# A planned order of work laid out anew: the self-attention block of the loop, half blocks of values, and an earlier transpose in the second step

## The chip, the core and the metric

The kernel runs on one core of a Trainium2 chip. The metric is the device time of one launch in microseconds. TensorE does the matrix products and transposes, VectorE (DVE) and ScalarE (ACT) read its PSUM banks, GpSimd (POOL) works on SBUF alone, SyncE (SP) issues most DMAs. Each engine works through a queue of its own in order and is held by semaphore waits.

## The reference

For 64 sequences of 128 tokens by 128 features, in float32:

```
x = x + tanh(gx) * cross_attention(layernorm(x), ctx)      # 16 heads of 8, 120 context tokens
h = rms(layernorm(x)); q, k = rms by head; v = h @ wv.T    # causal self-attention, 16 heads of 8
ffn_x = layernorm(x) + self_attention(h) @ wo.T            # the first 32 output features set to 0
moe = sum of 4 experts, two of them chosen by gate         # the first 32 output features set to 0
x = x + tanh(gf) * (ffn_x + moe)
```

Expert 0 has one hidden layer, expert 1 a gated one, expert 2 three, expert 3 two. All experts are computed for all tokens and weighted by `gates`.

## The kernel before

The sequences are worked in 16 groups of 4 (`G = 4`, 512 tokens). Work on a group is cut into five parts that lie one group apart in a software pipeline: N (layer norm, cross queries, keys, values), A (cross attention), B (norm, self queries, keys, values), D (self attention, gate, first expert layers), M (second and later expert layers, store). A step t does N of group t+1, A of group t, B of t-1, D of t-2 and M of t-3. Steps -1 to 2 are the ramp, steps 3 to 14 are twelve rounds of one hardware loop (`LOOP = (3, NG - 1)`), step 15 follows the loop's order without part N, and steps 16 to 18 are the tail.

The order of a loop step is written out by hand as a list, `SCHEDULE = self_attention() + second_experts() + cross_attention() + first_experts()`. Each entry is (part, work, index, ring). Every engine walks the same list and picks out the works in which it has a share, so the list sets the order in all five queues. `ring` names the PSUM banks that a work takes in turn: "w" is four banks, "s2" and "f" are both the pair s2a and s2b, "pv" and "t" are one bank each. Before a work writes its bank, TensorE waits until the use before has been read out (`st.drains`).

The works that matter here:

- `exact` (s2): two products of exact scores for sequence b; ScalarE takes the exponential of each into `probs` (L951). For part D, GpSimd masks each pair of results (L818), after a small `tick` (L817).
- `estimate` (s1): four products into the four "w" banks at once (L1302, L1306); TensorE waits for all four banks first. VectorE reduces each to maxima (L1092). After the last estimate of a part, `mT` transposes the maxima (L1315), ScalarE copies them, and SyncE stores them into a row of the stacked queries (L676); the first exact score of that part waits for this DMA.
- `values` (pv): 32 small products for one sequence (L1363), which wait for the exponentials, in part D for the masks. After each second sequence come oT (transpose; VectorE divides, L1131, L1133), nT and wo (L1376; VectorE adds, L1148).
- `qk`, `squares`, `sums`, `root`, `scale`, `qT`, `kT` of part B: the products (L1274) are copied by ScalarE, squared by GpSimd (L829), summed by VectorE (L1067), rooted by ScalarE (L905), scaled by VectorE (L1071, L1073), transposed by TensorE (L1225), and split by ScalarE (L856, L861) and VectorE (L985, L993).
- `down`: sixteen products of an expert's last layer (L1389); VectorE adds them into `ym` in four instructions (L1121).
- `D out` is yb (L1155), `N stats` and `N norm` are the statistics and xn (L1007), with a power by GpSimd between them (L760).

Numbers such as D13 below mean part D, sequence 1, quarter 3. The ramp's steps have lists of their own: `third_group()` is step 1, `fourth_group()` is step 2 and takes its first half from `self_attention()` without part M.

## Time and profile before

| | us |
|---|---|
| median of 3 runs | 1071.3 (1071.01 to 1073.17) |
| the profiled execution's own time | 1074.17 |
| its span, first to last instruction | 1072.5 |
| TensorE busy in the span | 1009.0 (94%) |
| VectorE busy | 788.7 (74%) |
| ScalarE busy | 736.5 (69%) |
| GpSimd busy | 338.1 (32%) |

A round of the loop takes 62.5 to 62.7 us. TensorE's busy time counts the latency of products that overlap, so that a gap of some tenths between products may not show in it. An idle time in brackets is that of the engine just before the instruction, with what ended it.

### The profile page before, as it was taken

What the parts mean: (1) busy time and instruction counts of PE and PEld (TensorE: products, weight loads), DVE (VectorE), ACT (ScalarE), POOL (GpSimd) and SP (SyncE); (2) the same over time, 40 slices, a digit from 0 to 9 for tenths busy, and PEclk for the clock granted to TensorE, in tenths of its full rate; (3) what the DMA queues carried; (4) which work ended last, traced back from release to release, by engine and by line L of the source; (5) the groups of instructions that cost most, each with busy time, mean ns of one, the idle gap of its engine ahead of it and who ended that gap; (6) DMA issues with size and microseconds to landing.
All of it is one profiled execution on the core that took longest, in us unless ns stands there. A gap on an engine that the chain in (4) does not pass through costs nothing.

```text
span 1072.5 us, 26205 instructions
## 1 busy us (share of the span) xinstructions
PE 1009.0 (94%) x8649; PEld 627.7 (59%) x8649; DVE 788.7 (74%) x2172; ACT 736.5 (69%) x1334; POOL 338.1 (32%) x463
## 2 busy tenths in 40 slices
PE   6768799999999999999999999999999999999898
PEld 5445556556565655656565565656556565656565
DVE  8546878777877877787787778778777877774723
ACT  6465767676777767677776767777676777767453
POOL 5613424141422414142241414224141422404130
PEclk9868999999999999999999999999999999999999
DMA  7424432233342224334222443422244342221200
GB/s 233 127 72 158 133 104 89 88 130 128 115 134 96 87 88 130 128 115 135 97 86 88 130 128 115 135 96 87 88 130 128 115 135 96 82 79 49 83 1 20
DMA packets 77317, 114.28 MB, mean 107 GB/s; under 512 B 7776, under 2 KB 40160, under 8 KB 77152
## 3 DMA queue, kind: packets, MB, share of 16 engines
q1 hardware_dynamic: 76800, 111.53, 32.1%
q10 hardware_dynamic: 480, 2.26, 0.6%
q8 instruction: 23, 0.38, 0.1%
q14 instruction: 14, 0.11, 0.0%
HBM read 58.97 MB, written 53.74 MB: 105 GB/s over the span
## 4 chain that ended last, share of the span: by engine, by line
PE 65%; DVE 14%; ACT 11%; issue 6%; DMA 2%; SPq 1%; POOL 0%; ACTq 0%; DVEq 0%; POOLq 0%
PE ps_pv L1363 9%; PE ps_w L1389 9%; PE ps_s2a L1342 7%; PE ps_s2b L1342 5%; PE ps_s2a L1401 5%; PE ps_s2b L1408 4%; ACT probs L951 4%; PE ps_t L1225 4%; PE ps_w L1408 3%; PE ps_w L1274 3%; DVE mpadA L1092 3%; PE ps_t L1376 2%; PE ps_w L1225 2%; PE ps_w L1306 2%; PE ps_w L1302 2%
## 5 line engine op out<-in xcount | busy, mean ns | idle before, releaser
L951 ACT ACTIVATE probs<-ps_s2a 120x512 f32<-120x512 f32 (+1 forms) x256 | 153.4, 599 | 76.6 <-PE ps_s2a L1342 68.5
L1092 DVE TENSOR_REDUCE mpadB<-ps_w 128x4 f32<-128x512 f32 x240 | 148.8, 683 | 22.7 <-PE ps_w L1306 22.7
L1092 DVE TENSOR_REDUCE mpadA<-ps_w 128x4 f32<-128x480 f32 x224 | 131.5, 650 | 38.1 <-PE ps_w L1306 38.1
L951 ACT ACTIVATE probs<-ps_s2b 120x512 f32<-120x512 f32 (+1 forms) x256 | 153.5, 599 | 0.0
L818 POOL TENSOR_SCALAR_AFFINE_SELECT probs<-probs 128x1024 f32<-128x1024 f32 x128 | 139.8, 1092 | 0.0
L1389 PE MATMUL ps_w<-W,hid 128*128 128x96 f32 x976 | 121.3, 278 | 1.0 <-DVE split_k L985 0.9
L1389 PEld LDWEIGHTS ps_w<-W,hid 128*128 128x128 f32 x976 | 113.8, 192 | 10.4 <-issue 4.9
L786 POOL TENSOR_TENSOR rB<-vrB,neg_half 128x4 f32<-128x4 f32 x16 | 16.1, 1008 | 204.5 <-DVE veB L978 204.5
L1342 PE MATMUL ps_s2a<-qdA,kstA 128*120 128x512 f32 x128 | 70.2, 548 | 9.2 <-DMA qdA<-scratch_Aq 4.8
L1401 PE MATMUL ps_s2a<-hid,W 128*128 128x512 f32 x152 | 74.4, 604 | 0.0
L1121 DVE SCALAR_TENSOR_TENSOR ym<-ps_w,gates,ym 128x96 f32<-128x96 f32 x184 | 45.7, 311 | 38.6 <-PE ps_w L1389 38.6
L955 ACT ACTIVATE oT<-ps_pv 128x512 f32<-128x512 f32 x64 | 38.3, 598 | 50.9 <-PE ps_pv L1363 50.9
L1342 PE MATMUL ps_s2a<-qdB,kstB 128*128 128x512 f32 x128 | 64.6, 505 | 7.6 <-ACT probs L951 2.1
L1363 PE MATMUL ps_pv<-probs,VA 120*18 120x128 f32 x2048 | 71.2, 282 | 0.0
L947 ACT ACTIVATE hid<-ps_s2a 128x512 f32<-128x512 f32 x73 | 43.7, 599 | 40.0 <-PE ps_s2a L1401 30.9
L1363 PE MATMUL ps_pv<-probs,VB 128*18 128x128 f32 x2048 | 68.4, 274 | 0.0
L1363 PEld LDWEIGHTS ps_pv<-probs,VA 120*18 120x18 f32 x2048 | 51.9, 100 | 24.2 <-issue 22.9
L817 POOL TENSOR_TENSOR tick<-one 128x1 f32<-128x1 f32 x128 | 24.9, 194 | 117.5 <-ACT probs L951 113.2
L1363 PEld LDWEIGHTS ps_pv<-probs,VB 128*18 128x18 f32 x2048 | 50.5, 97 | 17.2 <-issue 16.9
L958 ACT ACTIVATE onT<-ps_t 128x256 f32<-128x256 f32 x64 | 24.5, 384 | 51.6 <-PE ps_t L1225 51.6
L1342 PE MATMUL ps_s2b<-qdA,kstA 128*120 128x512 f32 x128 | 59.3, 463 | 0.0
L825 POOL TENSOR_TENSOR ym<-yb,one 128x128 f32<-128x128 f32 x16 | 6.4, 398 | 166.2 <-DMA out_x<-ym 166.2
(279 smaller groups left out, 2170.3 us busy)
## 6 DMA issues: line engine op xcount, KB each, us to landing
scratch_Aq<-split_q SPq DMA_DIRECT2D x48, 256.0 KB, 2.4
qdA<-scratch_Aq SPq DMA_DIRECT2D x64, 192.0 KB
scratch_Bq<-split_q SPq DMA_DIRECT2D x48, 256.0 KB, 2.4
scratch_Bk<-split_k SPq DMA_DIRECT2D x48, 256.0 KB, 2.9
qdB<-scratch_Bq SPq DMA_DIRECT2D x64, 192.0 KB
kstB<-scratch_Bk SPq DMA_DIRECT2D x64, 192.0 KB
scratch_Ak<-split_k SPq DMA_DIRECT2D x48, 240.0 KB, 2.3
kstA<-scratch_Ak SPq DMA_DIRECT2D x64, 180.0 KB
```

The costliest lines, as they stand in the source:

```text
L818: pool.affine_select(out=tile, in_=tile, compare_op=ALU.is_ge, fill=0.0, base=0, pattern=[[0, 2 * HT], [1, P]], channel_multiplier=-1).the ...
L947: nc.scalar.activation(hid[:, HID_AT[index[0]] + index[1], :], bank[:], ACT.Gelu).then_inc(done, 1)
L951: nc.scalar.activation(probs[0:k, slot_of(part, *index), :], bank[0:k, :], ACT.Exp, scale=SCALE if part == "A" else 1.0).then_inc(done, 1)
L955: nc.scalar.activation(oT[:], bank[:], ACT.Copy).then_inc(done, 1)
L1092: nc.vector.tensor_reduce(pair[:, :, c, b % 2] if halves else mneg[p][:, :, c, b], bank[:, 0:HT * k].rearrange("p (h k) -> p h k", h=HT), ...
L1121: ins = nc.vector.scalar_tensor_tensor(out=ym[:, b, KEEP:P], in0=bank[:, b * UP:(b + 1) * UP], scalar=gates[:, b, e:e + 1], in1=y[:, b, KE ...
L1225: ins = nc.tensor.transpose(psum[st.bank[key]][:, b * P:(b + 1) * P], of(b), identf[:])
L1342: mm(o, kst[p][:, c, b * k:(b + 1) * k], qd[p][:, :, c, b * P:(b + 1) * P], start=True, stop=True).then_inc(done, 1)
L1363: ins = mm(psum[st.bank[last]][32 * j:32 * j + VS, at:at + P], VB[p][0:k, first:first + VS], probs[0:k, slot_of(part, b, c), j * P:(j + 1) ...
L1389: ins = mm(bank[:, b * UP:(b + 1) * UP], hid[:, HID_AT[h] + k, b * P:(b + 1) * P], w[f"down{index[1]}"][:, k * UP:(k + 1) * UP], start=k = ...
L1401: ins = mm(bank[:], w[name][:, k * HID + c * P:k * HID + (c + 1) * P], hid[:, HID_AT[h] + k, :], start=k == 0, stop=k == chunks[-1])
L1408: mm(bank[:], w[name][:, c * P:(c + 1) * P], xfT[:], start=True, stop=True).then_inc(done, 1)
```

## The change

Nothing is computed differently, and no instruction is added but for the waits of the half blocks. What changes is order:

- `values` of part D is split into `early_values` (quarters 0 and 1) and `late_values` (quarters 2 and 3), 16 products each, laid between other works.
- `down(0)` is split into `head(0)` (sequences 0 and 1) and `rest(0)`; VectorE still adds all four in one go, after `rest`.
- In `self_attention()` the estimates A0 and A1 come later, and A2 moves behind the output product wo0, into `second_experts()`; so does the whole of e2_l2.
- In `second_experts()` the B transposes qT and kT come before the second output product wo1, `out` and `squares` of part D; in VectorE's queue the splits of queries and keys therefore come before wo1's addition and yb.
- Step 1 begins with B's hT, ahead of the first exact scores of A. In step 2, estimate A2 comes behind wo0 as in the loop, and A3 behind `scale` and oT1.

```
 def self_attention():
-    return (... exact("D", 0, 0) + one("B", "hT") + down(1) + exact("D", 0, 2)
-            + one("B", "qk", 0) + one("B", "qk", 1) + one("B", "qk", 2) + one("B", "qk", 3)
-            + exact("D", 1, 0) + estimate("A", 0) + exact("D", 1, 2)
-            + one("B", "squares", 0, None) + values("D", 0)
-            + exact("D", 2, 0) + estimate("A", 1) + exact("D", 2, 2)
-            + values("D", 1) + one("B", "sums", 0, None) + down(0)
-            + exact("D", 3, 0) + one("D", "oT", 0, "t") + estimate("A", 2) + exact("D", 3, 2)
-            + one("A", "base", 0, None) + values("D", 2) + one("D", "nT", 0, "t") + one("B", "root", 0, None))
+    return (... exact("D", 0, 0) + one("B", "hT") + down(1)
+            + exact("D", 0, 2) + one("B", "qk", 0) + one("B", "qk", 1) + early_values("D", 0)
+            + exact("D", 1, 0) + one("B", "qk", 2) + one("B", "qk", 3) + late_values("D", 0)
+            + exact("D", 1, 2) + one("B", "squares", 0, None) + estimate("A", 0) + early_values("D", 1)
+            + exact("D", 2, 0) + head(0) + late_values("D", 1)
+            + exact("D", 2, 2) + one("B", "sums", 0, None) + rest(0) + one("D", "oT", 0, "t")
+            + exact("D", 3, 0) + early_values("D", 2) + estimate("A", 1) + one("D", "nT", 0, "t") + late_values("D", 2)
+            + exact("D", 3, 2) + one("A", "base", 0, None) + one("B", "root", 0, None))
 def second_experts():
-    return (fill("M", "e2_l2", 0) + one("D", "wo", 0, "t") + one("B", "scale", 0, None) + fill("M", "e2_l2", 1)
-            + estimate("A", 3) + values("D", 3) + fill("M", "e3_up", 0) + one("D", "oT", 1, "t") + fill("M", "e3_up", 1)
-            + one("N", "stats", 0, None)
-            + one("D", "nT", 1, "t") + one("A", "mT") + fill("M", "e2_l3", 0) + one("N", "norm", 0, None) + one("D", "wo", 1, "t")
-            + one("D", "out", 0, None) + one("B", "qT") + one("B", "kT") + one("D", "squares", 0, None)
-            + fill("M", "e2_l3", 1, "w"))
+    return (one("D", "wo", 0, "t") + early_values("D", 3) + estimate("A", 2) + fill("M", "e2_l2", 0) + one("B", "scale", 0, None)
+            + late_values("D", 3) + fill("M", "e2_l2", 1) + estimate("A", 3) + fill("M", "e3_up", 0) + one("D", "oT", 1, "t")
+            + fill("M", "e3_up", 1) + one("N", "stats", 0, None) + one("A", "mT") + fill("M", "e2_l3", 0) + one("D", "nT", 1, "t")
+            + one("N", "norm", 0, None) + one("B", "qT") + one("B", "kT") + one("D", "wo", 1, "t")
+            + one("D", "out", 0, None) + one("D", "squares", 0, None) + fill("M", "e2_l3", 1, "w"))
 def third_group():
-    return (exact("A", 0, 0) + exact("A", 0, 2) + one("A", "mL", 0, "t") + exact("A", 1, 0) + values("A", 0) + one("B", "hT")
-            + exact("A", 1, 2) + one("B", "qk", 0) ... + one("B", "qk", 3)
-            + one("B", "squares", 0, None) + one("B", "copy", 0, None)
+    return (one("B", "hT") + exact("A", 0, 0) + exact("A", 0, 2)
+            + one("B", "qk", 0) ... + one("B", "qk", 3) + one("A", "mL", 0, "t")
+            + exact("A", 1, 0) + exact("A", 1, 2) + one("B", "squares", 0, None) + one("B", "copy", 0, None) + values("A", 0)
             + exact("A", 2, 0) + one("B", "sums", 0, None) + one("B", "root", 0, None) + exact("A", 2, 2)
 def fourth_group():
-            + one("D", "wo", 0, "t") + estimate("A", 3) + values("D", 3) + one("D", "oT", 1, "t") + one("A", "mT")
-            + one("B", "scale", 0, None) + one("D", "nT", 1, "t") + one("N", "stats", 0, None) + one("D", "wo", 1, "t")
+            + one("D", "wo", 0, "t") + early_values("D", 3) + estimate("A", 2) + one("B", "scale", 0, None) + late_values("D", 3)
+            + one("D", "oT", 1, "t") + estimate("A", 3) + one("A", "mT") + one("D", "nT", 1, "t") + one("N", "stats", 0, None) + one("D", "wo", 1, "t")
```

The new functions (`head` writes half of the bank that `down` 0 takes, and signals nothing; `rest` signals):

```
+def early_values(part, b):
+    return values(part, b, 0, PACK)
+def late_values(part, b):
+    return values(part, b, PACK, NT)
+HEADED = (0,)
+def head(e):
+    return one("M", "head", e, None)
+def rest(e, ring="w"):
+    return fill("M", "down", e, ring)
+def down(e, ring="w"):
+    return (head(e) if e in HEADED else []) + rest(e, ring)
...
-                        for b in range(G):
+                        for b in range(0 if work == "head" or e not in HEADED else G // 2, G // 2 if work == "head" else G):
```

The tail's lists call `down` under its new form, in the order they had.

## Rows read from the trace of the kernel before

**Rows 1.** The page, its first line
```profile
span 1072.5 us, 26205 instructions
...
```

**Rows 2.** One whole step of the loop: us, busy us by engine, TensorE's clock, DMA
```profile
...
403.07:465.61 62.54, 61.21 (x536) 38.03 (x536) 48.85 (x136) 45.40 (x84) 19.37 (x25) 1.00 0.34 111
...
```

**Rows 3.** Timeline of TensorE in the loop step from 403.07: start, us, [idle before]
```profile
...
409.63 0.50 PE L1342 MATMUL ps_s2a<-qdB,kstB 128*128 128x512 f32 x1
...
417.93 0.38 PE L1306 MATMUL ps_w<-kdA,qTbA 32*128 32x480 bf16 x4 [0.32 <-DVE ym L1121]
...
428.04 0.44 PE L1225 MATMUL ps_t<-identf,on 128*128 128x128 f32 x2
...
430.57 1.04 PE L1225 MATMUL ps_w<-identf,qk 128*128 128x128 f32 x8
...
438.67 0.40 PE L1302 MATMUL ps_w<-causal_k,causal_q 32*128 32x512 bf16 x4
...
```

**Rows 4.** Timeline of VectorE, the same step
```profile
...
414.89 1.21 DVE L1067 TENSOR_REDUCE hs<-sq 128x128 f32<-128x1024 f32 x1
416.79 0.99 DVE L1121 SCALAR_TENSOR_TENSOR ym<-ps_w,gates,ym 128x96 f32<-128x96 f32 x4 [0.69 <-PE ps_w L1389]
...
422.52 0.36 DVE L1148 TENSOR_TENSOR x<-ps_t,x 128x192 f32<-128x192 f32 x1 [1.76 <-PE ps_t L1376]
...
424.92 2.34 DVE L1092 TENSOR_REDUCE mpadA<-ps_w 128x4 f32<-128x480 f32 x4
...
430.52 1.11 DVE L1007 TENSOR_SCALAR xn<-xt,mvA,rsA 128x128 f32<-128x128 f32 x4 [1.13 <-POOL rsA L760]
...
432.02 1.54 DVE L1155 SCALAR_TENSOR_TENSOR yb<-x,tg,xc 128x512 f32<-128x512 f32 x1
...
434.15 0.73 DVE L985 SCALAR_TENSOR_TENSOR split_k<-ps_w,vc,split_k 128x512 fp32r<-128x512 f32 x1
...
436.66 0.99 DVE L1121 SCALAR_TENSOR_TENSOR ym<-ps_w,gates,ym 128x96 f32<-128x96 f32 x4
439.30 2.49 DVE L1092 TENSOR_REDUCE mpadB<-ps_w 128x4 f32<-128x512 f32 x4 [1.65 <-PE ps_w L1306]
```

**Rows 5.** Timeline of GpSimd, the same step
```profile
...
411.68 1.09 POOL L818 TENSOR_SCALAR_AFFINE_SELECT probs<-probs 128x1024 f32<-128x1024 f32 x1
412.74 1.89 POOL L829 TENSOR_TENSOR sq<-qk 128x1024 f32<-128x1024 f32 x1
...
```

**Rows 6.** Timeline of ScalarE, the same step
```profile
...
435.43 0.60 ACT L951 ACTIVATE probs<-ps_s2a 120x512 f32<-120x512 f32 x1
...
```

**Rows 7.** Timeline of all engines in the second step (t=1)
```profile
...
53.22 1.11 DVE L1032 TENSOR_SCALAR hb<-x,mvB,rB 128x128 f32<-128x128 f32 x4 [1.13 <-POOL rB L786]
...
58.90 1.12 PE L1225 MATMUL ps_w<-identf,hb 128*128 128x128 f32 x4
...
63.39 1.89 POOL L829 TENSOR_TENSOR sq<-qk 128x1024 f32<-128x1024 f32 x1 [9.22 <-ACT qk L896]
...
68.87 0.95 DVE L1071 RECIPROCAL hr<-hr 128x128 f32<-128x128 f32 x1
...
71.13 1.12 PE L1225 MATMUL ps_w<-identf,qk 128*128 128x128 f32 x4 [5.38 <-DVE qk L1073]
```

**Rows 8.** Timeline of all engines in the third step (t=2)
```profile
...
107.60 1.21 DVE L1067 TENSOR_REDUCE hs<-sq 128x128 f32<-128x1024 f32 x1
...
112.64 2.35 DVE L1092 TENSOR_REDUCE mpadA<-ps_w 128x4 f32<-128x480 f32 x4
...
115.71 0.55 SPq L676 DMA_DIRECT2D qdA<-mTA  x1
...
118.73 0.75 PE L1342 MATMUL ps_s2a<-qdA,kstA 128*120 128x512 f32 x1 [1.24 <-issue]
...
126.24 0.40 PE L1302 MATMUL ps_w<-causal_k,causal_q 32*128 32x512 bf16 x4 [0.33 <-ACT xnT L870]
...
```

**Rows 9.** Busy time and clock in eight microseconds of the third step
```profile
...
116.00:124.00 8.00, 5.40 (x26) 4.39 (x26) 7.01 (x23) 5.95 (x10) 2.03 (x2) 0.79 0.16 54
...
```

More of the change, by code:

```diff
@@ L89, in estimate, with values @@
     return [(part, "s1", (b, c), rings[c]) for c in range(NT)]
-def values(part, b):
-    return [(part, "pv", (b, c), "pv" if b % 2 and c == NT - 1 else None) for c in range(NT)]
+def values(part, b, first=0, last=NT):
+    return [(part, "pv", (b, c), "pv" if b % 2 and c == NT - 1 else None) for c in range(first, last)]
+def early_values(part, b):
+    return values(part, b, 0, PACK)
+def late_values(part, b):
+    return values(part, b, PACK, NT)
 def one(part, work, index=0, ring="w"):
@@ new lines, in head @@
+def head(e):
[4 more added lines that the diff above has]
+    return (head(e) if e in HEADED else []) + rest(e, ring)
+def self_attention():
+    return (one("N", "load", 0, None) + one("N", "ctx", 0, None) + exact("D", 0, 0) + one("B", "hT") + down(1)
+            + exact("D", 0, 2) + one("B", "qk", 0) + one("B", "qk", 1) + early_values("D", 0)
[5 more added lines that the diff above has]
+            + exact("D", 3, 2) + one("A", "base", 0, None) + one("B", "root", 0, None))
@@ L236, in last_self_keys @@
             + one("D", "squares", 2, None) + estimate("B", 1) + fill("M", "e2_l3", 1)
[L237 to L238 removed]
+            + down(2, "pv") + estimate("B", 2) + one("D", "norm", 2, None) + one("B", "init", 0, None) + one("B", "copy", 0, None)
+            + one("D", "xfT", 0, "t") + down(3, "pv") + one("M", "store", 0, None) + one("B", "v", 0, "f") + one("D", "logits", 0, "t")
             + fill("D", "e1_w1", 0) + fill("D", "e1_w2", 0) + one("D", "keep", 0, None) + estimate("B", 3)
@@ L261, in last_experts @@
 def last_experts():
-    return (fill("M", "down", 1, "t") + fill("M", "e2_l2", 0) + fill("M", "e2_l2", 1) + down(0) + fill("M", "e2_l3", 0) + fill("M", "e2_l3", 1)
+    return (down(1, "t") + fill("M", "e2_l2", 0) + fill("M", "e2_l2", 1) + down(0) + fill("M", "e2_l3", 0) + fill("M", "e2_l3", 1)
             + fill("M", "e3_up", 0, "w") + fill("M", "e3_up", 1, "w") + down(2) + down(3) + one("M", "store", 0, None))
@@ L1378, in step @@
                         ins.then_inc(done, 1)
-                    elif work == "fill" and index[0] == "down":
-                        h = DOWN_OF[index[1]]
-                        if index[1] in (0, 1):
-                            sources = st.settled(*(("f",) if st.parts == "M" and index[1] == 1 else ("w", "f")))
-                        else:
-                            sources = st.drains([("M", "fill", (h, k)) for k in range(2)])
-                        for b, v in merged(sources, st.drains([], key)):
-                            pe.wait_ge(drained[b], v)
-                        for b in range(G):
+                    elif work == "head" or work == "fill" and index[0] == "down":
+                        e = index if work == "head" else index[1]
+                        use, h = ("M", "fill", ("down", e)), DOWN_OF[e]
+                        if work == "head" or e not in HEADED:
+                            if e in (0, 1):
+                                sources = st.settled(*(("f",) if st.parts == "M" and e == 1 else ("w", "f")))
+                            else:
+                                sources = st.drains([("M", "fill", (h, k)) for k in range(2)])
+                            for b, v in merged(sources, st.drains([], use)):
+                                pe.wait_ge(drained[b], v)
+                        for b in range(0 if work == "head" or e not in HEADED else G // 2, G // 2 if work == "head" else G):
                             for k in range(2):
-                                ins = mm(bank[:, b * UP:(b + 1) * UP], hid[:, HID_AT[h] + k, b * P:(b + 1) * P],
-                                         w[f"down{index[1]}"][:, k * UP:(k + 1) * UP], start=k == 0, stop=k == 1)
-                        ins.then_inc(done, 1)
+                                ins = mm(psum[st.bank[use]][:, b * UP:(b + 1) * UP], hid[:, HID_AT[h] + k, b * P:(b + 1) * P],
+                                         w[f"down{e}"][:, k * UP:(k + 1) * UP], start=k == 0, stop=k == 1)
+                        if work == "fill":
+                            ins.then_inc(done, 1)
                     elif work == "fill" and index[0] in ("e2_l2", "e2_l3", "e3_up"):
```

7 lines of the change are left out of this document (1 added, 6 removed).

## The prediction

> **What bounds the kernel now.** I read the page first: the span is 1072.5 us [rows 1]. Then the windows, step by step: a loop step takes 62.5 us, TensorE is busy for 61.2 of them at full clock, VectorE for 48.9 [rows 2]. That looks like a TensorE bound, but the busy time counts overlapping latencies, so I read the chain of waits through one step and then the four timelines beside each other. In the stretch that the change lays out anew, TensorE stops for others: for the addition of `down` 0 before estimate A2, for the divided output before nT1, and only then runs on to qT and to the first causal estimate B0 [rows 3]. VectorE stops twice, 0.69 us before ym and 1.76 us before wo0's addition, and 1.65 us before B0's maxima [rows 4]. So neither is full; the step's length is set by a chain that changes engines. From B0 onwards the order is unchanged, and what the change does to a loop step is how much earlier or later B0 starts than at 438.67 [rows 3].
>
> **The loop step, worked through in the new order.** I lay the new order on the old clock, with the step's first exact score at 403.07.
>
> TensorE first. Before D12 it now has all 32 value products of sequence 0 and no estimate: the values cost 1.0 us, the estimate and a stop 0.5, so D12 starts at about 410.1 and not at 409.63 [rows 3]. D13 follows it at streaming distance, so its mask starts only 0.3 us later than at 411.68, near 412.0. GpSimd's squares stand behind that mask, and come at 413.0 for 412.74 [rows 5]; they take 1.89 us and end at 414.9. `sums` on VectorE waited for VectorE itself before; it now waits for the squares and starts at 414.94 for 414.89 [rows 4]. The early start of the values costs nothing there, since A0's four maxima are done by 413.4.
>
> From here VectorE is the chain, because A1 as well as A2 and A3 now stand behind `sums`. The distances from start to start, all from [rows 4] or the neighbouring starts of the same timeline: sums 1.14, ym 0.91 (416.79 to the next start), division and product of oT0 0.73, maxima A1 2.26 (the 2.34 of four less their overlap with the next), and so A1 is read at 420.0. TensorE can issue A2 only when A1's last bank is free, which costs VectorE 0.35, then A2 2.26, addition of wo0 and the scaling together 2.40 (422.52 to 424.92). That is 414.94 + 1.14 + 0.91 + 0.73 + 2.26 + 0.35 + 2.26 + 2.40 = 424.99 for A3, against 424.92. VectorE's two stops of 0.69 and 1.76 us are gone, and one more set of maxima, 2.26 us, has taken their place. The masks, exponentials and head/rest of `down` 0 lie beside this: late D1 is free at 413.1, `rest` is filled at 415.3, while VectorE gets to ym at 416.1. If that cover went, each tenth late at ym would be a tenth at B0. TensorE meanwhile waits some 0.4 us for the mask before early D1, 0.6 for ym before A1 (D2's first half and D3 are queued behind it only in part), 0.4 for nT0; it is off the chain, so these cost nothing now.
>
> A3 to xn is 5.60 us (424.92 to 430.52), the same works in the same order, so xn starts at 430.6. On TensorE, mT now stands before e2_l3 and nT1 behind it. mT waits for A3's maxima until 427.4; then 1.72 for e2_l3's first half and 0.27 for nT1 bring qT to 429.55, against 430.57 [rows 3]: one microsecond earlier, since wo1 has moved behind. ScalarE's four casts end 0.9 us earlier, at 432.7, and its first exponential of A00 comes at 434.7 for 435.43 [rows 6], there held by e2_l3's second half, whose products end at 432.6.
>
> VectorE then does the splits before wo1's addition and yb. xn ends at 431.7, the query split runs to 432.3, and the key split must wait for ScalarE until 432.73. After it: key split to ym 2.51 (434.15 to 436.66), addition and yb 0.36 + 1.54, ym 0.99, which is 432.73 + 2.51 + 1.90 + 0.99 = 438.1; B0 waits for ym's bank and starts at 438.3. TensorE and ScalarE alone would have allowed 438.1. So a loop step gains 438.67 - 438.3 = 0.4 us. No DMA decides: the store of mT's row is issued at about 428.0 and takes 3.0 us as in [rows 8] (115.71 to 118.73), A00 comes at 432.6; the load of x is issued 0.3 us later behind `base` and has until 428. The bounds: if ScalarE's casts or the start of A2 come sooner than I have it, 0.6 (TensorE's and ScalarE's limit); if each stop adds a tenth or the squares are late by 0.3, nothing or a loss of 0.1. Twelve rounds and step 15 make thirteen: -4.8 us, between -8 and +1.5.
>
> **Step 2.** It takes the same list without M. The anchor is the same: squares at 105.6, sums at 107.6 [rows 8]. Before, all maxima but A3's were done or next; A3's were read from 112.64 for 2.35 us, to 115.0, ahead of the scaling. Now VectorE has after sums: oT0 0.73, A1 2.26, addition 0.3 and a gap of 0.35, A2 2.26, scaling 2.12, oT1 0.73, A3 2.34, from 107.6 + 1.14. That ends at 119.8, later by 4.8. Here no e2_l2 or e3_up fills TensorE, and mT, its DMA and A00 follow at the distances of before, 0.72 to the issue and 3.02 to A00: 123.6 for 118.73. The B transposes are queued behind A00 on TensorE, and everything up to B0 at 126.24 behind them; ScalarE's and VectorE's splits had some slack there (they waited for xn), which gives back 0.3 to 0.6. I take +4.5, between +2.5 and +6.
>
> Clock: in 116 to 124 it averages 0.79 of full [rows 9], and the exact score A00 took 0.75 us. The new order leaves TensorE idle for some 4 us before mT, so the low level (1.2 GHz) may reach on into B0. The Trainium skill, "TensorE: Matmul & The Clock Gate", section "HAM oscillation", says that idle stretches between bursts of matmuls bring the half clock back and each must be paid anew. By that rule step 2 would cost more than these 4.5 us; by the rows, where the stretch was at 0.79 anyway, it costs no more. The sum goes by the rows; the rule is a rival below.
>
> **Step 1.** hT can start when hb ends, 53.22 + 1.11 = 54.33; it started at 58.90 [rows 7]. Now A00, ready at 53.19, is queued behind it, and so are A's exponentials, by 1.4 us. The four qk end near 61.2, squares at 61.65 for 63.39. But the root stands on ScalarE behind the exponentials of A20 and A21, and these behind mL's row, whose transpose has moved behind qk. I get A21's exponential to 65.9, a table load of 1.28 and the root to 67.6, the reciprocal at 67.65 for 68.87, and qT as much before 71.13. The gain is 1.2 us, between 0 and 2.
>
> **Other edits.** `down` in its new form issues the same products in the tail: nothing. Split values add waits that are long met: nothing.
>
> **Sum.** -4.8 + 4.5 - 1.2 = -1.5 us, on the span 1072.5, so 1071.0. The profiled execution took 1074.17 in all, 1.7 above its span and 2.9 above the median of the timed runs, 1071.3; taken off that median, the forecast is 1069.8 us. A measurement of this kernel tells about 0.2%, 2.1 us, from no change: this is a change of 0.14%, within it.
>
> **Rivals.**
> - *VectorE does not bind the loop step.* If the wait for ScalarE before the key split vanishes and the estimates are issued early, a step gains 0.6 to 0.9. For it: qT is a whole microsecond earlier, and VectorE stood idle 1.65 us before B0. Against: the order puts A1 behind sums. With 0.75 a step, 9.8, and steps 1 and 2 as above: 1064.8 us.
> - *The squares set a later chain.* Slower: GpSimd's mask of D13 stands before the squares, and the squares before the masks of D2. If TensorE reaches D13 0.8 us later than before instead of 0.3 (each half block restarting after its wait), sums starts 0.5 later, the step loses 0.1, and with steps 1 and 2 the time is 1071.3 + 1.3 + 3.3 = 1075.9. It decides from a delay of 0.4 us, where the gain of a step is gone.
> - *The clock in step 2.* As the skill's page would have it: nT1, wo1, A00, qT and the estimate at half speed cost 1.5 more, 1071.3 us.
> - *Nothing at all in the loop* is no case of its own; it lies between the first two.
>
> **How the numbers follow.** Forecast, 0.40: 1067.5 to 1072.5, of this 0.12 faster, 0.27 the same, 0.01 slower. No VectorE bound, 0.32, all faster. Late squares, 0.20: 0.18 slower, 0.02 the same. Clock, 0.08: 0.01 faster, 0.05 the same, 0.02 slower. Together faster 0.45, same 0.34, slower 0.21. The range leaves a tenth on each side: the first rival's 1064.8 with its larger half, and the slower one's centre: 1063.5 to 1075.5. For the likeliest alone it is 1067.5 to 1072.5.
>
> **What would show it.** In the changed loop step: the distance from the first exact score to B0, 35.2 us for 35.6; VectorE without a stop of over 0.4 us from sums to A3's end, and its ym of `down` 2 ending just before B0; sums about 11.9 us after the step's first score. In step 2: A00 nearly 5 us later after sums than 11.1 us, with VectorE solid before it. In step 1: hT at once after hb, and ScalarE's root as the last thing before the scaling. The prediction is wrong if B0 waits for something else than ym, if sums slips by 0.4 us or more, or if step 2 doesn't move.

## The result and the profile of the changed kernel

The changed kernel is slower: 1082.95 us, median of 4 runs (1081.08 to 1084.22), against 1071.78 for the kernel before (4 runs, 1071.01 to 1073.17), a ratio of 1.0098 with an interval of 1.0082 to 1.0114. The forecast was 1069.8 within 1063.5 to 1075.5, so the time lies 7.5 us outside the range. The page of the changed kernel's profiled execution, 1081.08 us in all:

```profile
span 1079.2 us, 26181 instructions
...
PE 1009.3 (94%) x8649; PEld 622.4 (58%) x8649; DVE 791.3 (73%) x2172; ACT 733.6 (68%) x1334; POOL 339.0 (31%) x463
...
```

One loop step, from its first exact score to that of the next, the two steps of the ramp from the start of one hT to the start of the next, and the eight microseconds of [rows 9] (us, busy us by engine, the clock, DMA):

```profile
...
405.21:468.31 63.10, 61.43 (x536) 37.70 (x537) 49.06 (x136) 45.21 (x84) 19.40 (x25) 1.00 0.35 111
52.09:91.21 39.12, 28.63 (x245) 17.37 (x246) 24.50 (x66) 23.15 (x44) 5.91 (x5) 0.83 0.26 87
91.21:152.66 61.45, 50.55 (x453) 30.04 (x453) 44.40 (x116) 39.58 (x75) 20.04 (x25) 0.89 0.36 116
116.00:124.00 8.00, 6.48 (x26) 5.17 (x25) 4.41 (x18) 5.86 (x11) 2.09 (x2) 0.54 0.02 4
...
```

The loop step took 62.54 us [rows 2] and takes 63.10, step 2 took 56.13 from hT to hT (96.28 to 152.41) and takes 61.45. From the end of hb to the next hT, step 1 took 41.95 and takes 39.18. From the hT of step 3 to that of step 16, thirteen intervals of which eleven grew by 0.52 to 0.58 and the two at the ends by 0.3, the sum is 6.5 us. Over the two profiled executions: 6.5 + 5.3 - 2.8 - 2.3 (the ramp up to hb, where the orders are the same) - 0.1 (the tail) = 6.7 us, the difference of the spans. The ramp's 2.3 and part of the 2.8 are scatter between executions (below); with step 1 at the 1.2 us that its order gives and the ramp at nothing, the parts make 10.6; the medians differ by 11.2.

TensorE in the loop step (start, us, what ended the stop before it):

```profile
...
412.54 0.50 PE L1364 MATMUL ps_s2a<-qdB,kstB 128*128 128x512 f32 x1
...
419.72 0.38 PE L1328 MATMUL ps_w<-kdA,qTbA 32*128 32x480 bf16 x4 [0.42 <-DVE ym L1143]
420.35 0.44 PE L1247 MATMUL ps_t<-identf,on 128*128 128x128 f32 x2 [0.25 <-DVE on L1155]
...
422.92 0.38 PE L1328 MATMUL ps_w<-kdA,qTbA 32*128 32x480 bf16 x4
...
427.63 0.38 PE L1328 MATMUL ps_w<-kdA,qTbA 32*128 32x480 bf16 x4
...
430.45 0.33 PE L1337 MATMUL ps_w<-identf,mpadA 128*128 128x128 f32 x1
...
432.65 1.04 PE L1247 MATMUL ps_w<-identf,qk 128*128 128x128 f32 x8
...
441.36 0.40 PE L1324 MATMUL ps_w<-causal_k,causal_q 32*128 32x512 bf16 x4 [0.28 <-DVE ym L1143]
...
```

VectorE, the same step:

```profile
...
417.45 1.22 DVE L1089 TENSOR_REDUCE hs<-sq 128x128 f32<-128x1024 f32 x1 [1.48 <-POOL sq L851]
...
420.21 2.35 DVE L1114 TENSOR_REDUCE mpadA<-ps_w 128x4 f32<-128x480 f32 x4
...
423.33 2.35 DVE L1114 TENSOR_REDUCE mpadA<-ps_w 128x4 f32<-128x480 f32 x4 [0.51 <-PE ps_w L1328]
...
428.04 2.35 DVE L1114 TENSOR_REDUCE mpadA<-ps_w 128x4 f32<-128x480 f32 x4 [0.24 <-PE ps_w L1328]
...
435.85 0.75 DVE L1007 SCALAR_TENSOR_TENSOR split_k<-ps_w,vc,split_k 128x512 fp32r<-128x512 f32 x1 [0.41 <-ACT split_k L883]
...
437.95 1.63 DVE L1177 SCALAR_TENSOR_TENSOR yb<-x,tg,xc 128x512 f32<-128x512 f32 x1
...
440.31 0.99 DVE L1143 SCALAR_TENSOR_TENSOR ym<-ps_w,gates,ym 128x96 f32<-128x96 f32 x4
...
```

GpSimd, the same step:

```profile
...
415.52 1.90 POOL L851 TENSOR_TENSOR sq<-qk 128x1024 f32<-128x1024 f32 x1
...
```

The step begins at 405.21, and all distances below are from that start (403.07 before). D12 comes at 7.33 (forecast 7.03), the squares at 10.31 (9.67 before [rows 5]; forecast 9.93), sums at 12.24 (11.82 before [rows 4]; forecast 11.87), A3's maxima at 22.83 (21.85 before; forecast 21.92), qT at 27.44 (27.50 before [rows 3]; forecast 26.5), B0 at 36.15 (35.60 before; forecast 35.2). So the handing over of A3 is 0.9 us later than I had it, and everything behind it by as much: from A3's maxima to B0 the forecast had 13.3 us and the trace has 13.32. The second thing to see is TensorE between nT0 at 420.35 and A3's estimate at 427.63: no row there has a stop, while VectorE waits 0.51 and 0.24 us for the products of A2 and A3. The chain that I had put on VectorE lies on TensorE there.

Step 1, all engines:

```profile
...
64.89 0.40 ACT L927 ACTIVATE hr<-hs,rms_eps 128x128 f32<-128x128 f32 x1
...
65.32 0.95 DVE L1093 RECIPROCAL hr<-hr 128x128 f32<-128x128 f32 x1 [0.30 <-ACT hr L927]
...
67.59 1.09 PE L1247 MATMUL ps_w<-identf,qk 128*128 128x128 f32 x8 [2.47 <-DVE qk L1095]
...
```

Step 2, all engines:

```profile
...
102.76 1.22 DVE L1089 TENSOR_REDUCE hs<-sq 128x128 f32<-128x1024 f32 x1 [1.46 <-POOL sq L851]
...
113.10 2.34 DVE L1114 TENSOR_REDUCE mpadA<-ps_w 128x4 f32<-128x480 f32 x4
...
115.50 0.48 PE L1337 MATMUL ps_w<-identf,mpadA 128*128 128x128 f32 x1 [4.20 <-DVE mpadA L1114]
...
119.10 0.75 PE L1364 MATMUL ps_s2a<-qdA,kstA 128*120 128x512 f32 x1 [1.05 <-issue]
...
126.48 0.40 PE L1324 MATMUL ps_w<-causal_k,causal_q 32*128 32x512 bf16 x4 [0.31 <-ACT xnT L892]
...
```

### The profile page after: what moved, and what is told of

It reads as the page before. It is cut to its first block, busy times and chain, and to the rows that moved or that the text cites. A ratio compares the mean times of both kernels' runs of the same rounds, so it can differ in the third digit from the quotient of the medians.

```text
span 1079.2 us, 26181 instructions
## 1 busy us (share of the span) xinstructions
PE 1009.3 (94%) x8649; PEld 622.4 (58%) x8649; DVE 791.3 (73%) x2172; ACT 733.6 (68%) x1334; POOL 339.0 (31%) x463
## 4 chain that ended last, share of the span: by engine, by line
PE 62%; DVE 17%; ACT 9%; issue 8%; POOL 3%; DMA 0%; DVEq 0%; ACTq 0%; POOLq 0%
PE ps_pv L1385 10%; PE ps_w L1413 6%; PE ps_s2a L1364 6%; PE ps_s2a L1426 5%; PE ps_s2b L1433 4%; PE ps_s2b L1364 3%; PE ps_t L1247 3%; PE ps_s2b L1426 3%; PE ps_w L1433 3%; PE ps_w L1296 3%; DVE mpadA L1114 3%; PE ps_w L1328 2%; DVE ym L1143 2%; POOL sq L851 2%; ACT probs L973 2%
## 5 line engine op out<-in xcount | busy, mean ns | idle before, releaser
L1385 PE MATMUL ps_pv<-probs,VB 128*18 128x128 f32 x2048 | 79.9, 277 | 2.1 <-POOL probs L840 2.0
L1385 PE MATMUL ps_pv<-probs,VA 120*18 120x128 f32 x2048 | 69.0, 276 | 0.1
L1385 PEld LDWEIGHTS ps_pv<-probs,VB 128*18 128x18 f32 x2048 | 45.9, 97 | 37.9 <-issue 22.8
L969 ACT ACTIVATE hid<-ps_s2b 128x512 f32<-128x512 f32 x60 | 35.8, 597 | 30.2 <-PE ps_s2b L1426 26.1
L1364 PE MATMUL ps_s2b<-qdA,kstA 128*120 128x512 f32 x128 | 56.2, 439 | 0.0
```

The source lines that it names most:

```text
L969: nc.scalar.activation(hid[:, HID_AT[index[0]] + index[1], :], bank[:], ACT.Gelu).then_inc(done, 1)
L1364: mm(o, kst[p][:, c, b * k:(b + 1) * k], qd[p][:, :, c, b * P:(b + 1) * P], start=True, stop=True).then_inc(done, 1)
L1385: ins = mm(psum[st.bank[last]][32 * j:32 * j + VS, at:at + P], VB[p][0:k, first:first + VS], probs[0:k, slot_of(part, b, c), j * P:(j + 1) ...
```

## The experiments

Each kernel is read by the same clock: the distance from one hT on TensorE to the next, which within one execution repeats to some hundredths of a microsecond over the inner steps of the loop, where the interval of a ratio is some 2 us wide. "Stops" are the stretches of TensorE's timeline between the step's first exact score and B0 in which no matmul runs, added up; what is left of that distance I call TensorE's own time; a wait shorter than the latency of the matmul before it hides in there (exact scores that start 0.49 us apart and not 0.34), so it is no fixed amount of work: late_estimates below, which cuts no block, has 1.0 us more of it than tail_on_before. The columns are good to 0.02 us.

```
kernel             loop step   first score to B0 = stops + own   step 2
before                 62.55       35.61           0.98   34.63   56.13
changed                63.09       36.14           1.16   34.98   61.45
tail_on_before         62.35       35.42           0.99   34.43   56.09
whole_values           63.19       36.26           1.43   34.83   60.78
halves_of_1_2          63.09       36.17           1.46   34.71   61.96
estimates_forward      63.03       36.10           1.29   34.81   58.15
late_estimates         64.70       37.79           2.33   35.46   56.12
```

**Which part costs.** step1_alone is the kernel before with the new third_group and nothing else.

> The kernel before with the new order of step 1 alone (hT first). In the changed kernel the stretch from the end of hb in step 1 to hT of step 2 was 39.2 us against 41.9, so the new order of step 1 is expected to give 2.8 us by itself: 1069, ratio 0.9975. If that gain needs the changed loop, or was the chance of one execution, the ratio is 1.000. My prediction had 1.2 us for it. All loop steps must stay at 62.55 us.

It took 1069.67 us, ratio 0.9984 (0.997 to 0.9999), and its loop step is 62.56. The new step 1 gains 1 to 1.7 us (0.1 to 3.2 by the interval), and not the 2.8 of the two profiles. The end of hb to qT takes 15.72 us in it and 15.56 in the changed kernel, and 16.2 to 16.8 in the four kernels with the old step 1; all fifteen with the new one lie between 14.2 and 15.8, with 15.4 in the middle, so the order gives about 1.1 us there. From qT to the next hT the four take 22.6, 24.3, 24.4 and 25.2 us: that stretch is scatter.

step2_of_before is the changed kernel whose fourth_group has the old order (ramp_self_attention is the old list under a new name, and the lines behind it are the old ones too):

```
-    return (one("D", "mL", 0, "t") + of_parts("NABD", self_attention())
+    return (one("D", "mL", 0, "t") + of_parts("NABD", ramp_self_attention())
```

> The changed kernel with step 2 in the order of before (self-attention and what follows it up to A00), loop and step 1 changed. If step 2 costs 5.3 us as hT to hT of step 3 says (61.45 against 56.13), the time is 5 us under the changed kernel's, 1078, ratio to before about 1.0045 to 1.005. If the loss of step 2 is only the time won in step 1 that is given back at the next DMA or at the start of the loop, it stays near 1083. Loop steps stay at 63.09 us.

1079.31 us, ratio 1.0072 (1.0049 to 1.0094), step 2 at 56.18 for 61.45, the loop step unchanged at 63.09. Step 2 costs 3.6 us by the medians, 2.8 by the ratios, whose intervals are some 2 us wide to each side, and 5.3 by the profiles; the loop costs the rest. Step 2 scatters too: with the old order it took 56.1 to 56.2 us in six kernels and 57.2 in two (step1_and_tail, wo1_between), with the changed one 61.4, 61.45 and 62.15.

step2_a3_first keeps the new step 2 and puts A3 ahead of the scaling and of oT1 in it:

> The changed kernel with one thing moved, in step 2 only: estimate A3 ahead of scale and oT1, as before. If step 2's 5.3 us come through A3's maxima, mT, its DMA and A00, the stretch hT to hT of step 2 shrinks from 61.4 by the scaling and the division that A3 no longer waits for, by 2 to 3 us. If they come from the first half of the step (half blocks, masks), it stays at 61.

1084.35 us, ratio 1.0122 (1.0108 to 1.0137); step 2 takes 60.49, 1.0 less and not 2 to 3. mT comes 2.2 us earlier behind sums, but nT1 and wo1 are queued ahead of A00 on TensorE and wait for the divided output, which the scaling has moved back; so A00 comes only 0.94 us earlier behind sums. The time itself shows no gain.

**The new tail.** tail_on_before is the kernel before with the change's tail of second_experts alone:

```
-            + one("N", "stats", 0, None)
-            + one("D", "nT", 1, "t") + one("A", "mT") + fill("M", "e2_l3", 0) + one("N", "norm", 0, None) + one("D", "wo", 1, "t")
-            + one("D", "out", 0, None) + one("B", "qT") + one("B", "kT") + one("D", "squares", 0, None)
+            + one("N", "stats", 0, None) + one("A", "mT") + fill("M", "e2_l3", 0) + one("D", "nT", 1, "t")
+            + one("N", "norm", 0, None) + one("B", "qT") + one("B", "kT") + one("D", "wo", 1, "t")
+            + one("D", "out", 0, None) + one("D", "squares", 0, None)
```

> The kernel before with one part of the change alone: in second_experts the tail from stats on in the new order (mT, e2_l3's first half, nT1, norm, qT, kT, wo1, out). The block of exact scores and the estimates A0 to A3 stay where they were, steps 1 and 2 too. Theory T (the new tail by itself is right as the prediction had it, and what the change loses is that the block hands over A3 about 1.0 us later): A3's maxima stay 21.85 us behind the step's first exact score, mT and qT follow them at the changed kernel's distances (2.41 and 4.61 us), so qT at 26.5 and B0 8.7 us later at 35.2; a loop step takes 62.15 us for 62.55 and the kernel 5 us less, about 1066. Rival O (the tail order itself costs: the splits ahead of wo1's addition lengthen qT to B0 from 8.10 to 8.71 us, and qT does not come earlier, since xn, which waits for GpSimd's root, stands before the splits): a loop step of 62.9 to 63.1 us, the kernel 5 to 7 us longer than before. Between: no change, 62.5 to 62.6.

The loop step is 62.35 us, 0.20 shorter; 1069.4 us, ratio 0.9988 (0.9975 to 1.0001), so the time alone does not tell it from no change, and the step does. Its step from 521.96, TensorE:

```profile
...
548.67 1.04 PE L1224 MATMUL ps_w<-identf,qk 128*128 128x128 f32 x8
...
557.38 0.40 PE L1301 MATMUL ps_w<-causal_k,causal_q 32*128 32x512 bf16 x4 [0.27 <-DVE ym L1120]
...
```

qT is at 26.71 and B0 at 35.42; A3's maxima stayed at 21.85. The tail does what the prediction said, at half the size. By the table the gain is in TensorE's own time, 34.43 for 34.63, and not in its stops. wo1_first asks the reverse, the changed kernel with the old tail:

```
-            + fill("M", "e3_up", 1) + one("N", "stats", 0, None) + one("A", "mT") + fill("M", "e2_l3", 0) + one("D", "nT", 1, "t")
-            + one("N", "norm", 0, None) + one("B", "qT") + one("B", "kT") + one("D", "wo", 1, "t") + one("D", "out", 0, None)
+            + fill("M", "e3_up", 1) + one("N", "stats", 0, None) + one("D", "nT", 1, "t") + one("A", "mT") + fill("M", "e2_l3", 0)
+            + one("N", "norm", 0, None) + one("D", "wo", 1, "t") + one("D", "out", 0, None) + one("B", "qT") + one("B", "kT")
```

> The changed kernel with the second half of second_experts in the order of before: nT1 before mT, wo1's addition and yb before the splits of queries and keys. Theory A, the late maxima (A1 behind sums, A3 begins 0.98 us later from the step's start than before) are what costs, and qT before wo1 hides part of it: a loop step gets longer than 63.09 by 0.2 to 0.45, 3 to 6 us in all. Theory B, the place of the splits costs, since the key split waits 0.41 us for ScalarE with yb and ym behind it: a loop step gets shorter by up to 0.4, 5 us in all.

63.52 us a step, 1089.79 us in all, ratio 1.0168 (1.0144 to 1.0191). So the four corners are 62.55 (old, old), 62.35 (old block, new tail), 63.52 (new block, old tail), 63.09 (both new): the new block costs 0.74 with the new tail and 0.97 with the old one, which is the 0.98 by which A3 is late.

**Is VectorE the chain up to A3?** half_read takes work from VectorE alone: its maxima of A1 read half of the keys, so the stabilizer of that sequence's scores comes from half of them.

```
-    bank[:, 0:HT * k].rearrange("p (h k) -> p h k", h=HT),
+    bank[:, 0:HT * k].rearrange("p (h k) -> p h k", h=HT)[:, :, 0:k // 2 if (part, b) == ("A", 1) else k],
```

> The changed kernel, but VectorE reads only the first 60 of 120 keys for the four maxima of estimate A1, which takes about 1.1 us out of its queue between sums and A2 (so the maxima of sequence 1 are those of half its keys). Theory V, VectorE's queue alone is the chain from sums to A3, as the prediction had it: a loop step gets shorter by 0.5 to 0.9 us, 7 to 12 us in all. Theory T, TensorE's own run from nT0 to A3 (7.3 us without a stop, against 6.65 in my sum) is the chain, and VectorE waits for A2's and A3's products (0.51 and 0.24 us): the step stays within 0.1 us of 63.09.

The step stays at 63.08 (1081.04 us, ratio 1.0101, 1.0085 to 1.0117). VectorE in its step from 468.33:

```profile
...
483.32 1.34 DVE L1114 TENSOR_REDUCE mpadA<-ps_w 128x4 f32<-128x240 f32 x4
485.58 0.36 DVE L1170 TENSOR_TENSOR x<-ps_t,x 128x192 f32<-128x192 f32 x1 [0.91 <-PE ps_t L1398]
486.44 2.35 DVE L1114 TENSOR_REDUCE mpadA<-ps_w 128x4 f32<-128x480 f32 x4 [0.51 <-PE ps_w L1328]
...
491.15 2.35 DVE L1114 TENSOR_REDUCE mpadA<-ps_w 128x4 f32<-128x480 f32 x4 [0.23 <-PE ps_w L1328]
...
```

A1's maxima take 1.34 us for 2.34, the microsecond turns into a stop of 0.91 before wo0's addition, and A3's maxima start at 22.82, where they were. So VectorE's queue does not set A3 here: TensorE's run from nT0 to A3 does, and nT0 itself stands behind sums, ym and the division on VectorE.

**The value products in halves.** whole_values is the changed kernel with every `early_values` left out and every `late_values` whole.

> The changed kernel with the value products of part D whole, all at the place of the later half; the rest of the layout kept. Theory A1, the entries between half blocks of values and exact scores make TensorE late (an exact score after small value products takes 0.43 and not 0.23, half a block 0.56 and not 0.50), so that squares and the estimates A2 and A3 come late: a step gets 0.3 to 0.45 us shorter, 4 to 6 us in all, to about 1078. Theory A2, only the order on VectorE (A1 behind sums) counts: the step stays within 0.1 us of 63.09.

63.19 us a step, 1080.64 us, ratio 1.0089 (1.0066 to 1.0112): the halves don't cost more than they fill. What one costs by itself shows two_splits, the kernel before with two blocks of A cut where TensorE doesn't wait:

```
-    values("A", 2) + one("D", "logits")
+    values("A", 2, 0, PACK) + one("D", "logits") + values("A", 2, PACK, NT)
-    fill("D", "e1_w2", 0, "w") + values("A", 3)
+    values("A", 3, 0, PACK) + fill("D", "e1_w2", 0, "w") + values("A", 3, PACK, NT)
```

> The kernel before with two blocks of value products in cross_attention and first_experts cut in halves round another work (A2 round the logits, A3 round e1_w2's first half), where TensorE runs without a stop; nothing else moved. Theory H (a half block costs TensorE 0.1 to 0.3 us each time it is restarted, also where nothing waits): a loop step grows by 0.2 to 0.5 us, the kernel by 3 to 7 us. Rival (the cut costs nothing, the exact scores were longer only since they stood behind small products): within 0.05 us a step, the kernel the same within 1 us.

The step is 63.08 us, 0.53 more, and the kernel 1079.63, ratio 1.008 (1.006 to 1.01): two cuts cost as much as the whole change of the block and tail. A2's block and what follows it, whole in the kernel before:

```profile
...
574.16 1.07 PE L1363 MATMUL ps_pv<-probs,VA 120*18 120x128 f32 x32
575.16 1.05 PE L1264 MATMUL ps_w<-W,xfT 128*128 128x4 f32 x8
576.08 0.41 PE L1225 MATMUL ps_t<-identf,on 128*128 128x128 f32 x2
576.33 1.02 PE L1408 MATMUL ps_w<-xfT,W 128*128 128x512 f32 x2
...
```

and cut in two_splits:

```profile
...
574.78 0.63 PE L1363 MATMUL ps_pv<-probs,VA 120*18 120x128 f32 x16
575.35 1.05 PE L1264 MATMUL ps_w<-W,xfT 128*128 128x4 f32 x8
576.33 0.63 PE L1363 MATMUL ps_pv<-probs,VA 120*18 120x128 f32 x16
576.89 0.44 PE L1225 MATMUL ps_t<-identf,on 128*128 128x128 f32 x2
577.17 1.02 PE L1408 MATMUL ps_w<-xfT,W 128*128 128x512 f32 x2
...
```

From the start of the block to that of the product behind nT it takes 2.39 us for 2.17. The 32 products took 1.00, the two sixteens 0.57 and 0.56; the work behind each is slower too, the logits by 0.06 here. The other cut costs 0.22 on its own stretch and 0.10 ahead of it. I take 0.22 to 0.27 us a cut.

halves_of_1_2 is the changed kernel with sequences 0 and 3 whole at their late places.

> The changed kernel with the value products of sequences 0 and 3 whole at the places of their late halves; those of 1 and 2 stay in halves. Theory H (each split costs TensorE 0.22 us, and both of these stand in runs that set the chain: sequence 0's before the mask that releases the squares, sequence 3's between nT0 and A3): sums 0.22 us sooner, 12.02 us behind the step's first exact score, A3's maxima 0.44 us sooner, at 22.4, and a loop step of 62.65 us for 63.09. Rival L (the estimates' later places are the whole loss): a step of 63.05 to 63.1.

Not a hundredth: 63.09 us a step (1082.02 us, ratio 1.0087, 1.0067 to 1.0107). Half of the theory held, sums at 12.02 as expected. But now TensorE stops for VectorE before A2; its step begins at 534.45:

```profile
...
549.37 0.44 PE L1247 MATMUL ps_t<-identf,on 128*128 128x128 f32 x2 [0.25 <-DVE on L1155]
...
551.72 0.38 PE L1328 MATMUL ps_w<-kdA,qTbA 32*128 32x480 bf16 x4 [0.27 <-DVE mpadA L1114]
...
556.87 0.38 PE L1328 MATMUL ps_w<-kdA,qTbA 32*128 32x480 bf16 x4
...
```

A3's estimate is at 22.42, as in the changed kernel (427.63 - 405.21): the 0.22 won at sums is lost from nT0 on, 7.50 us for 7.28. The early half of sequence 3 (0.56) is gone from that run, the whole block is 0.44 longer than the late half was, and 0.34 comes back between wo0 and A2, as a wait for A1's maxima. That is also why half_read found nothing: with the halves in, VectorE is ready for A2 some 0.2 us before TensorE asks for it, and whoever shortens TensorE's run by more meets VectorE's (17.27 us from the step's start to A2's estimate here, released by A1's maxima, with sums 0.22 earlier, for 17.71 in the changed kernel). From A2's estimate to A3's, TensorE needs 5.15 us with a whole block between e2_l2's halves (1.91 + 1.00 + 1.92 + 0.32); my sum had only VectorE's 4.66 there.

**The estimates' places.** late_estimates has, on tail_on_before, the change's later places of A0 to A3 and wo0 alone; value blocks, down 0 and the four qk are whole where they were.

> The kernel before with the new tail (a loop step of 62.35 us) and the estimates A0 to A3 and wo0 at the later places of the change, but all value products whole and the qk blocks where they were; step 2 as before. Theory H (half blocks alone are the loss): a loop step within 0.1 us of 62.35. Rival L (the later places alone, since TensorE's own run from nT0 to A3 then stands behind the wait for ym): 62.7 to 63.1 us. Between the two, 62.5, both have a share.

64.70 us a step, 2.35 more than tail_on_before (1099.74 us, ratio 1.0254, 1.0229 to 1.0278), beyond both theories. TensorE in its step from 539.04:

```profile
...
545.60 0.50 PE L1353 MATMUL ps_s2a<-qdB,kstB 128*128 128x512 f32 x1 [0.49 <-ACT probs L962]
...
549.31 0.49 PE L1353 MATMUL ps_s2a<-qdB,kstB 128*128 128x512 f32 x1 [0.45 <-ACT probs L962]
...
554.44 0.38 PE L1317 MATMUL ps_w<-kdA,qTbA 32*128 32x480 bf16 x4 [0.25 <-DVE ym L1132]
...
557.32 0.68 PE L1387 MATMUL ps_t<-W,onT 128*128 128x96 f32 x4 [0.47 <-ACT onT L969]
...
```

Where an estimate stood between two exact scores, TensorE now waits for ScalarE to drain a bank; where wo0 had e2_l2 ahead of it, it waits for the cast onT. The estimates were the filling. So what the change does to the block is to take this filling out, at 2.35 us a step, and to put other filling in (halves of values, of qk and of down 0), which gives 1.6 back. Which of these gives it was asked by two more of the changed kernel, qk_together (four qk ahead of sequence 0's first values) and whole_down (down 0 whole at the place of its second half):

> The changed kernel with the four qk products together again behind qk 0 and 1, ahead of sequence 0's first value products; all else as changed. If the qk pairs fill the times in which TensorE would wait for ScalarE to drain the exact scores' banks (0.49 and 0.45 us in late_estimates), a loop step grows by 0.4 to 1.0 us from 63.09; if the value halves fill them as well, within 0.1 us.

> The changed kernel with down 0 whole at the place of its second half. If its first half fills a wait for ScalarE's drains or for the mask ahead of sequence 1's second value products, a loop step grows by 0.3 to 0.6 us from 63.09, and ym comes later behind sums; if sums and the squares ahead of it are what ym waits for anyway, within 0.1 us.

63.17 and 63.18 us a step, in one execution each (1084.23 and 1082.06 us): each alone is worth 0.1, like the value halves in whole_values. That they stand in for one another is the likeliest reading, since without all three it is 64.70; no run takes out two of them, and in whole_values the whole blocks still stand where the late halves did.

estimates_forward keeps the halves and puts the estimates back (A0 ahead of D12, A1 ahead of sums, A2 and A3 one place forward, mT two blocks forward, stats ahead of oT1):

> The half blocks of the change kept, but all four estimates one place forward: A0 ahead of D12, A1 ahead of sums, A2 and A3 where the change has A1 and A2, mT two blocks earlier. If the places of the estimates are what costs the change 0.54 us a step, and the half blocks cost little, a step takes 62.2 to 62.6 us, at or under the 62.55 of before, and the whole comes to 1064 to 1072. If the half blocks cost by themselves, it stays at or above 62.9.

63.03 us a step (1078.0 us in all, ratio 1.0077, 1.0063 to 1.009, with a step 2 of 58.15). A3's maxima start at 18.99 there, 3.8 us earlier, and B0 moves by 0.04. VectorE from 402.53:

```profile
...
421.52 2.35 DVE L1114 TENSOR_REDUCE mpadA<-ps_w 128x4 f32<-128x480 f32 x4 [0.51 <-PE ps_w L1328]
...
427.10 0.87 DVE L990 BATCH_NORM_STATS2 stA<-xt 128x6 f32<-128x128 f32 x4 [1.11 <-DMA xt<-in_x]
...
431.96 0.75 DVE L1007 SCALAR_TENSOR_TENSOR split_q<-ps_w,qns,split_q 128x512 fp32r<-128x512 f32 x1 [1.12 <-ACT split_q L883]
433.12 0.75 DVE L1007 SCALAR_TENSOR_TENSOR split_k<-ps_w,vc,split_k 128x512 fp32r<-128x512 f32 x1 [0.41 <-ACT split_k L883]
...
```

The time is waited off before stats, for the load of x, and before the splits, for ScalarE's casts, which wait for qT. And qT, at 27.39 for 26.71 in tail_on_before, starts without a stop: TensorE has 0.98 us of stops ahead of it (0.65 there) and 26.41 of its own time (26.06 there). So of the 0.68 us a half is own time and a half is stops, the largest of them 0.41 before A1, for A0's maxima. That the own time is that of the four cuts is not shown: the halves alone on tail_on_before were not run. a1_early (A1 before sums but A0 still behind D12, down 0 whole) went the other way:

> The changed kernel with estimate A1 back ahead of sums (behind D20 and D21), the rest kept; down 0 is whole. If it is A1's place behind sums that costs, a step gets shorter by 0.9 or more. If the loss lies in A0's late start (VectorE is idle 3.7 us before it), A1's maxima now push sums and ym later by 0.7 instead, and the step changes by -0.2 to +0.4 us.

64.40 us a step, 1099.02 us, ratio 1.0258 (1.0243 to 1.0273), outside both theories. The trace names it: its two estimates stand so near to each other that the second waits for the maxima of the first.

```profile
...
557.66 0.39 PE L1328 MATMUL ps_w<-kdA,qTbA 32*128 32x480 bf16 x4 [1.30 <-DVE mpadA L1114]
...
```

**Toward a better kernel.** wo1_between tried qT ahead of wo1 but wo1's addition ahead of the key split, with the new step 1:

> Not a part of the change, a try at an order that keeps what is good in both: the kernel before with the new step 1, and in second_experts mT one place earlier (before e3_up's second half and stats), nT1 as before, qT ahead of wo1 but wo1's addition and yb ahead of the key split. If xn on VectorE bounds qT to B0 as in the kernel before, a loop step stays within 0.1 us of 62.55 and the kernel is that of the new step 1 alone, 1069.7; if qT's place behind wo1 was what held it, a step gains up to 0.5 us, the kernel 6 us more, about 1064.

62.54 us a step, 1069.02 us, ratio 0.9975 (0.9963 to 0.9986): the new step 1 and nothing more. step1_and_tail is tail_on_before with the new step 1, e2_behind_kT the same with `fill("M", "e2_l3", 0)` behind `one("B", "kT")`:

> The two parts that gained, on the kernel before: the new step 1 and the new tail of second_experts. If they add up: a loop step of 62.35 us, step 1 39.1 us, and 13 times 0.20 with 1.4 for step 1, 4.0 us less than before, a ratio of 0.996. If step 1's gain was only chance of one comparison: 0.9975.

> step1_and_tail with e2_l3's first half on TensorE behind kT instead of ahead of nT1. If the casts on ScalarE and the splits and ym on VectorE bound B0 (its last wait in the tail alone was 0.27 us for ym), qT comes 1.4 us earlier and TensorE becomes the bound: B0 0.25 us earlier, a loop step of 62.1 us, another 3 us off the kernel. If nT1's wait for the divided output, now with nothing to fill it, or the exact score behind e2_l3 eats it: 62.3 to 62.5.

1067.82 us, ratio 0.9957 (0.994 to 0.9974), loop step 62.36, and 1067.93, ratio 0.9971 (0.9954 to 0.9988), loop step 62.30. Both beat both kernels, by 3 to 4.6 us against the one before; between the two no difference can be told in the time, the step of the second is 0.05 us shorter and not 0.25. Its qT does come 1.5 us earlier (25.24 us behind the first score for 26.71), but the same work of TensorE still stands ahead of B0, at 35.36 for 35.42.

## Why the prediction was wrong

**The loop step (-4.8 forecast, +6.5 to +7 measured).** The step that failed is "From here VectorE is the chain", and with it, of TensorE, "it is off the chain, so these cost nothing now". Point by point: "D12 starts at about 410.1" came 0.30 later. The two half blocks ahead of it take 1.12 us for 1.0, and the four qk with D10's exact scores, now in two pairs with values behind each, 2.49 us for 2.34. I had written "Split values add waits that are long met: nothing", and looked at their waits, not at their issue. That made the squares and sums 0.37 late, nearly the 0.4 that the text named as its breaking point. From sums to A2's maxima I had 5.39 us and the trace has 5.88, from A2's to A3's 4.66 and 4.71: the first is TensorE's run behind nT0, with cut blocks in it, and it shows as VectorE's stop of 0.51 before A2's maxima, where "VectorE without a stop of over 0.4 us" was to be the sign. 0.37 + 0.49 + 0.05 = 0.91 at A3, where the forecast was 0.07 later than before. halves_of_1_2 shows that pricing the cuts right would not have been enough: VectorE's own chain and TensorE's 5.15 from A2 to A3 lead to the same 22.83.

Behind A3 the working held: A3 to B0 13.32 for 13.3, the key split held by ScalarE, ym just before B0. Taken alone, with A3 where it was, the tail gives 0.20 a step for the 0.4 I gave it. I had mT waiting for A3's maxima alone; in tail_on_before these end at 546.16 and mT starts at 546.62, behind e3_up's second half on TensorE (545.76), and from there to qT nothing stops.

The wider miss was at the start. I saw TensorE busy for 61.2 of 62.5 us [rows 2] and set the number aside because it counts overlapping latencies. But of the 35.6 us from the first score to B0, TensorE stood still for 0.98. A forecast of 35.2 with four cuts and more switches in it would have needed stops of 0.22 at the own time of 34.98 that the changed kernel has. Adding up TensorE's stops first would have shown that its visible waits could give a new order 1 us up to B0 at most, and that whatever lengthens its run by cuts or switches is paid out of that. It would not have given the loss as a number, since the own time itself moved between 34.43 and 35.46 with the order.

**Rivals.** "VectorE does not bind the loop step" was right in its title and wrong in its sign: from nT0 on TensorE does, and that costs. "The squares set a later chain" named the place of 0.37 of the 0.91; no rival had TensorE's own run in it. The clock: from 116 to 124 us it averages 0.54 of full for 0.79 before [rows 9], behind 4.20 us in which TensorE stood still, so its matmuls there ran almost wholly at the low level of 1.2 GHz. But from A00 to B0 it takes 7.38 us and took 7.51 [rows 8], so the rival's 1.5 us did not come: nT1 and wo1 ran while A00 waited for its transfer, and the eight products of qT and kT took 1.91 us in both kernels, since in the one before they ran at the low level too (0.54 from 119 to 122 us). The Trainium skill, "TensorE: Matmul & The Clock Gate", section "HAM oscillation", says that such a pause brings the low clock back; the trace agrees, and it cost nothing in this place.

**Step 2 (+4.5 forecast, +5.3 in the profiles, 3 to 4 us in the time).** Right. VectorE goes without a stop over 0.43 us from sums to A3's end, mT waits for it 4.20 us on TensorE, and A00 stands 16.34 us behind sums for 11.13 before: 5.2, of the "nearly 5" written. Sums itself is 0.23 later behind hT, and 0.13 comes back before B0; I had hoped for 0.3 to 0.6.

**Step 1 (-1.2 forecast, -1.4 in step1_alone's time).** Right in size and place: hb's end to qT 15.56 us for 16.80, 1.24 less, and the root on ScalarE is the last thing before the reciprocal at 65.32.

## What to carry to other kernels

When an engine is busy for 98% of a step, add up its stops before following any other engine's chain: they are all that its visible waits can give a new order, and each cut, switch or split in it is paid out of them. Waits shorter than a matmul's latency are not in that count; the 0.20 of the new tail was gained in TensorE's own time, where such waits lie. Work that merely stands between two dependent ones (here the estimates between exact scores) is filling; moving it away costs the waits that it covered, and they show only once it is gone. And where two chains end within a few tenths of each other, an experiment that shortens one and finds nothing proves only that the other is there too: shorten both before ruling one out.

## What the runs showed of the hardware

- Cutting 32 small matmuls (120x18 weights, 128 columns) into two sixteens with other matmuls between costs TensorE 0.13 us in the products themselves (0.57 + 0.56 for 1.00) and up to 0.14 more in what stands around them, though nothing waits: 0.53 us for two cuts. The Trainium skill, "TensorE: Matmul & The Clock Gate", section "Back-to-back issue gap", says that the spacing of such a stream is set by weight loads and matmuls together, pipelined. The trace here neither bears that out nor speaks against it: whether it is this pipeline that is filled anew at each switch no run shows.
- The same VectorE operation, yb (128x512), takes 1.63 us at 437.95 in the loop, beside GpSimd's xf of the same size at 438.00, and 0.75 at 125.63 in the changed kernel's step 2, where GpSimd only works on a tile of 128x4. No run takes xf away from beside it, so that xf is the cause is not shown.
- With the program unchanged up to there, the first hb ended between 51.0 and 55.0 us behind the start of the span in the nineteen traces, and the stretch behind qT of step 1 took 22.4 to 26.2 us. Steps of the loop differ by hundredths. A change of one loop step is read from the profile to some 0.05 us; one of the ramp is not.
